# A graph layer on one core: both halves of a pair side by side, eight groups in front, the difference begun on ScalarE and GpSimd

## What is computed

```
summed = segment_sum(x[src], dst)            # sum of the neighbours' rows
aggr   = summed / max(count, 1)
h      = aggr @ W_l.T + b_l + x @ W_r.T
h_norm = (h - mean over rows) * rsqrt(var over rows + 1e-5) * gamma + beta
out    = layernorm(x + relu(h_norm))
```

## Time and profile before

| what | value |
|---|---|
| median of 3 runs | 2656.01 us (2655.27 to 2657.59) |
| the profiled execution | 2652.04 us |
| its span, first to last instruction | 2650.3 us |
| PE busy | 1762.3 us, 66% |
| DVE busy | 1970.0 us, 74% |
| ACT busy | 1466.1 us, 55% |
| POOL busy | 1412.8 us, 53% |
| moved by DMA | 753.48 MB, mean 284 GB/s |

### The profile page before, as it was taken

How to read it: one execution, slowest core, us unless ns; L and a number is a source line. 1 busy time by engine, 2 the same in 40 slices (tenths; PEclk the granted TensorE clock), 3 DMA queues, 4 the chain that set the end, 5 groups by cost and what they waited for, 6 DMA issues and landing times.

```text
span 2650.3 us, 29633 instructions
## 1 busy us (share of the span) xinstructions
PE 1762.3 (66%) x9404; PEld 1421.6 (54%) x9404; DVE 1970.0 (74%) x3465; ACT 1466.1 (55%) x2847; POOL 1412.8 (53%) x688
## 2 busy tenths in 40 slices
PE   5589999999999999999999999997310000000000
PEld 4468777888887777888887777885200000000000
DVE  7735777788887777888887777885688766666666
ACT  3224444455555444555554444543369988888887
POOL 5334554545555555455555554554276656655554
PEclk9789999999999999999999999998655555555555
DMA  4256867888877877888877778888499999999998
GB/s 149 81 159 218 276 230 230 258 257 263 262 251 248 272 257 228 264 249 265 264 245 248 251 256 247 264 253 279 127 366 426 426 426 426 426 426 416 420 420 344
DMA packets 126763, 753.48 MB, mean 284 GB/s; under 512 B 22039, under 2 KB 22039, under 8 KB 66956
## 3 DMA queue, kind: packets, MB, share of 16 engines
q1 hardware_dynamic: 72940, 619.04, 60.7%
q0 software_dynamic: 53664, 132.51, 20.0%
HBM read 515.92 MB, written 246.22 MB: 288 GB/s over the span
## 4 chain that ended last, share of the span: by engine, by line
PE 49%; DMA 26%; DVE 11%; ACT 7%; issue 4%; POOL 2%; SPq 1%; DVEq 0%; POOLq 0%; ACTq 0%
DMA out<-hx 19%; PE pd L533 10%; PE pd L535 10%; PE pd L534 10%; PE pz L638 4%; PE pz L640 4%; PE pz L639 4%; DMA xf<-x,gi 4%; ACT hx L876 3%; ACT hx L886 2%; DVE x_lo L1032 2%; PE px L632 2%; DMA hs<-h_scratch 2%; DVE hot L1038 1%; PE pe L624 1%
## 5 line engine op out<-in xcount | busy, mean ns | idle before, releaser
L1368 POOL DMA_INDIRECT h_scratch<-zz,si x156 | 306.4, 1964 | 683.5 <-ACT zz L790 467.8
L533 PE MATMUL pd<-wc_hi,x_hi 128*128 128x512 f32 x1564 | 639.1, 409 | 40.8 <-POOL x_lo L1295 24.6
L534 PE MATMUL pd<-wc_lo,x_hi 128*128 128x512 f32 x1564 | 617.6, 395 | 7.0 <-issue 7.0
L535 PE MATMUL pd<-wc_hi,x_lo 128*128 128x512 f32 x1564 | 619.1, 396 | 0.0
L1391 POOL TENSOR_TENSOR hx<-hx,scale_b 128x2560 f32<-128x2560 f32 (+2 forms) x91 | 439.5, 4843 | 291.5 <-DMA hx<-h_scratch 250.0
L745 ACT ACTIVATE h_out<-pd 128x512 f32<-128x512 f32 x391 | 233.0, 596 | 403.5 <-PE pd L535 401.9
L533 PEld LDWEIGHTS pd<-wc_hi,x_hi 128*128 128x128 f32 x1564 | 298.3, 191 | 102.4 <-POOL x_lo L1295 24.6
L1320 POOL DMA_INDIRECT xn<-x,gi x156 | 310.3, 1989 | 47.7 <-issue 44.9
L534 PEld LDWEIGHTS pd<-wc_lo,x_hi 128*128 128x128 f32 x1564 | 298.8, 191 | 63.8 <-issue 7.3
L535 PEld LDWEIGHTS pd<-wc_hi,x_lo 128*128 128x128 f32 x1564 | 297.7, 190 | 66.0
L783 ACT ACTIVATE dT_hi<-px 128x512 fp32r<-128x512 f32 x156 | 93.3, 598 | 399.3 <-PE px L632 388.0
(11 more groups left out here) (214 smaller groups left out, 2939.3 us busy)
## 6 DMA issues: line engine op xcount, KB each, us to landing
raw<-xT_whole SPq DMA_DIRECT2D x78, 1280.0 KB
h_scratch<-h_out SPq DMA_DIRECT2D x78, 1280.0 KB
hs<-h_scratch SPq DMA_DIRECT2D x78, 1280.0 KB
hx<-x SPq DMA_DIRECT2D x78, 1280.0 KB, 20.6
hx<-h_scratch SPq DMA_DIRECT2D x77, 1280.0 KB, 15.4
out<-hx SPq DMA_DIRECT2D x77, 1280.0 KB, 18.1
xn<-x,gi POOLq DMA_INDIRECT x156
xf<-x,gi POOLq DMA_INDIRECT x156
```

What stands on the lines that cost most here:

```text
L533: pe.matmul(pd[i][0:n, :], hi, wc["hi"][:, kc, :], start=kc == 0, stop=False)
L534: pe.matmul(pd[i][0:n, :], hi, wc["lo"][:, kc, :], start=False, stop=False)
L535: last = pe.matmul(pd[i][0:n, :], lo, wc["hi"][:, kc, :], start=False, stop=kc == KC - 1)
L1368: pool.indirect_dma_start(out=h_dram[:, :], out_offset=by, in_=zz[:, h, :], in_offset=None, bounds_check=N + 2 * P - 1, oob_is_err=True, c ...
```

## The change

The diff does these things:

- `FRONT` becomes 8. GpSimd splits x for groups up to 8 instead of 4, the small steps of the front move to other places of `between` (rank_extras behind group 6's third product, which is the 33rd; sum_cover behind the 37th), and the turns 0 to 74 hold 341 products instead of 361.
- Each half has its own bank for spreading (`spread_to`) and for transposing (`turned`) and its own `dT_hi`, `dT_lo`. TensorE's order in a turn becomes: spread 0, product, spread 1, product, transpose 0, product, transpose 1, product, correction 0, product, slots, correction 1. The other engines' orders follow.
- `begin` leaves VectorE. ScalarE multiplies `xn` by `ndeg` in place (`scale_own`), and GpSimd adds it to `xf` (`begin`, behind add_z of pair u half 0).
- `copy_z` of half 1 moves to the head of the next turn on ScalarE.
- At the start, `src` and `dst` are loaded from ScalarE's queue, `dst` in rows with one neighbour to either side in place of three shifted copies. The first transposed rows are loaded before the weights, the low part of the weights moves from GpSimd to VectorE, and the first product starts block by block.

Parts that only rename or that belong to the path not taken are left out.

```diff
-FRONT = 4
+FRONT = 8
...
-        dT_hi = sr("dT_hi", [P, KC, P], F32R)
-        dT_lo = sr("dT_lo", [P, KC, P], F32R)
+        dT_hi = [sr(f"dT_hi{h}", [P, KC, P], F32R) for h in range(2)]
+        dT_lo = [sr(f"dT_lo{h}", [P, KC, P], F32R) for h in range(2)]
...
+        spread_to, turned = (pe_, p6), (px, p7)
...
+            load_xT(0)
             for s, w, m in ((s_wl_in, wT_l, 0), (s_wr_in, wT_r, 1)):
                 sp.dma_start(w_raw[:, m], w.rearrange("(c p) f -> p c f", p=P)).then_inc(s, 16)
-            load_xT(0)
...
-                (0, 4): (sum_blocks,),
-                (1, 0): (find_first,),
-                (1, 2): (lambda: pick_windows(0), lambda: pick_windows(1), lambda: pick_windows(2)),
-                (1, 3): (lambda: pick_windows(3), lambda: pick_windows(4)),
-                (1, 4): (lambda: pick_windows(5), lambda: pick_windows(6)),
-                (2, 0): (rank_slots,),
-                (2, 4): (rank_extras,),
-                (3, 3): (sum_cover,),
+                (1, 2): (sum_blocks,),
+                (1, 4): (find_first,),
+                (2, 3): [lambda a=a: pick_windows(a) for a in range(7)],
+                (2, 4): (rank_slots,),
+                (6, 2): (rank_extras,),
+                (7, 1): (sum_cover,),
...
-                if 2 * u + h > 0:
-                    pe.wait_ge(s_d, 2 * u + h)
+                if u > 0:
+                    pe.wait_ge(s_d, 2 * u + h - 1)
                 to = spread[:, h * P:(h + 1) * P]
-                pe.matmul(pe_[:], to, xe_hi[:], start=True, stop=False)
-                pe.matmul(pe_[:], to, xe_lo[:], start=False, stop=True).then_inc(s_e, 1)
+                pe.matmul(spread_to[h][:], to, xe_hi[:], start=True, stop=False)
+                pe.matmul(spread_to[h][:], to, xe_lo[:], start=False, stop=True).then_inc(s_e, 1)
...
                         spread_extras(a, 0)
                     plain(0)
                     if a is not None:
-                        transpose_difference(a, 0)
+                        spread_extras(a, 1)
                     plain(1)
                     if a is not None:
-                        correction(a, 0)
-                        spread_extras(a, 1)
+                        transpose_difference(a, 0)
                     plain(2)
                     if a is not None:
                         transpose_difference(a, 1)
                     plain(3)
                     if a is not None:
-                        correction(a, 1)
+                        correction(a, 0)
+                    plain(4)
                     if u + 2 < U:
                         fill_slots(u + 2)
-                    plain(4)
+                    if a is not None:
+                        correction(a, 1)
...
+            def scale_own(u, h):
+
+                act.wait_ge(s_gn[h], 16 * u + 16)
+                act.wait_ge(s_wgt, u + 1)
+                act.activation(xn[:, h, :], xn[:, h, :], ACT.Copy, scale=ndeg[:, u % 4, h:h + 1]).then_inc(s_own, 1)
...
-                    plain(tiles_at(u - 1)[TG - 1:])
+                    if pair_at(u - 1) is not None:
+                        copy_z(u - 1, 1)
                     if sp_ is not None:
                         for t in range(3, tiles_in(sp_)):
                             square(sp_, t)
+                    plain(tiles[0:2])
                     if a is not None:
                         difference_high(a, 0)
-                    plain(tiles[0:2])
+                    plain(tiles[2:3])
+                    if a is not None:
+                        difference_high(a, 1)
+                    plain(tiles[3:4])
+                    if pair_at(u + 1) is not None:
+                        extras_high(u + 1)
                     if a is not None:
                         copy_z(a, 0)
-                        difference_high(a, 1)
-                    plain(tiles[2:4])
                     if pair_at(u + 1) is not None:
-                        extras_high(u + 1)
+                        scale_own(u + 1, 0)
+                        scale_own(u + 1, 1)
+                    plain(tiles[4:])
                     if s is not None:
                         for t in range(min(3, tiles_in(s))):
                             square(s, t)
-                    if a is not None:
-                        copy_z(a, 1)
...
-            def begin(u, h):
-                dve.wait_ge(s_gn[h], 16 * u + 16)
-                dve.wait_ge(s_gf[h], 16 * u + 16)
-                dve.wait_ge(s_wgt, u + 1)
-                b = u % 2
-                dve.scalar_tensor_tensor(xf[:, b, h, :], xn[:, h, :], ndeg[:, u % 4, h:h + 1], xf[:, b, h, :],
-                                         ALU.mult, ALU.add).then_inc(s_t, 1)
...
                     if p is not None:
                         difference(p, 0)
+                    x_lows(0)
                     if 0 <= u + 2 < U:
                         one_hots(u + 2)
                     if p is not None:
-                        difference_low(p, 0)
-                    x_lows(0)
+                        difference(p, 1)
+                    x_lows(1)
                     if sums_at(u - 1) is not None:
                         take_squares(sums_at(u - 1))
-                    x_lows(1)
                     if p is not None:
-                        difference(p, 1)
+                        difference_low(p, 0)
                     x_lows(2)
                     if p is not None:
                         difference_low(p, 1)
+                    x_lows(3)
                     if sums_at(u) is not None:
                         take_sums(sums_at(u))
                     if pair_at(u + 1) is not None:
                         extras_low(u + 1)
-                        begin(u + 1, 0)
-                        begin(u + 1, 1)
-                    x_lows(3)
+                    x_lows(4)
                     if 0 <= u + 2 < U:
                         indices(u + 2)
...
+                def begin(u, h):
+                    b = u % 2
+                    pool.wait_ge(s_own, 2 * u + h + 1)
+                    pool.wait_ge(s_gf[h], 16 * u + 16)
+                    pool.tensor_tensor(xf[:, b, h, :], xf[:, b, h, :], xn[:, h, :], ALU.add).then_inc(s_t, 1)
...
                     if p is not None:
                         add_z(p, 0)
+                    if pair_at(u + 1) is not None:
+                        begin(u + 1, 0)
+                        begin(u + 1, 1)
```

More of the change, by code:

```diff
@@ L257, in bass_sage_batchnorm_residual_layernorm_kernel @@
         s_go = sem("gather_allowed")
-        s_t, s_xeh, s_xel, s_spread = (sem(n) for n in (
-            "differences_begun", "extras_hi", "extras_lo", "spread_ready"))
+        s_t, s_own, s_xeh, s_xel, s_spread = (sem(n) for n in (
+            "differences_begun", "own_rows_scaled", "extras_hi", "extras_lo", "spread_ready"))
         s_e, s_d, s_x, s_dh, s_dl, s_z, s_ze = (sem(n) for n in (
@@ L753, in copy_window, with blocks @@
                                    banks[a % 3][j][0:EB, 0:HALF], ACT.Copy).then_inc(s_got, 1)
+            act.dma_start(src_i[:, :, 0:EB], src.rearrange("(c b p) -> b c p", b=BP, p=EB)).then_inc(s_src, 16)
+            wide, block = EB + 2, BP * EB
+            def blocks(first, pattern):
+                return bass.AP(dst.tensor, first * EB - 1, [*pattern, [1, wide]])
+            act.wait_ge(s_pad, 1)
+            act.dma_start(dst_i[:, 1:BC - 1, 0:wide], blocks(BP, [[EB, BP], [block, BC - 2]])).then_inc(s_dst, 16)
+            act.dma_start(dst_i[1:BP, 0, 0:wide], blocks(1, [[EB, BP - 1]])).then_inc(s_dst, 16)
+            act.dma_start(dst_i[0:BP - 1, BC - 1, 0:wide], blocks((BC - 1) * BP, [[EB, BP - 1]])).then_inc(s_dst, 16)
+            act.dma_start(dst_i[0:1, 0, 1:wide], dst[0:EB + 1].rearrange("(o p) -> o p", o=1)).then_inc(s_dst, 16)
+            act.dma_start(dst_i[BP - 1:BP, BC - 1, 0:wide - 1], dst[E - EB - 1:E].rearrange("(o p) -> o p", o=1)).then_inc(s_dst, 16)
+            for kc in range(KC):
+                x_high(0, 0, kc)
             for kc in range(KC):
@@ L758, in _ @@
             for kc in range(KC):
-                x_high(0, 0, kc)
-            for kc in range(KC):
                 x_high(1, 1, kc)
-            between = {(1, 2): (0, 1, 2), (1, 3): (3, 4), (1, 4): (5, 6)}
+            between = {(2, 3): range(7)}
             for g in range(FRONT):
@@ L1155, in correct @@
                         dve.wait_ge(s_c[3], TG * g + t + 1)
[L1156 to L1157 removed]
+                        dve.tensor_tensor(dT_lo[0][:, :, 0:m], px[:].rearrange("p (c r) -> p c r", c=KC)[:, :, 0:m],
+                                          dT_hi[0][:, :, 0:m].bitcast(F32), ALU.subtract).then_inc(s_c[4], 1)
                         dve.wait_ge(s_c[5], TG * g + t + 1)
```

86 lines of the change are left out of this document (38 added, 48 removed).

## The result

The changed kernel takes 2673.96 us (median of 4 runs, 2671.69 to 2675.45), the kernel before 2655.64 us on the same chip (4 runs, 2653.08 to 2657.59). The ratio is 1.0069, with a 95% interval of 1.0051 to 1.0086. It is slower by 0.7%, where 2617 us was forecast.

A forecast was written before the change was run, and what follows sets the result against it. It took TensorE's 21.1 us a turn plus a ring of gathers through GpSimd to bound the kernel. Turns -54, front +20, tail -5 made -39, so 2617 us (2580 to 2650; 8 in 10: 2560 to 2662).

The forecast's parts named there:

- 75 x (22.02 - 21.3) = 54 us won: The 75 turns from pair 0 to pair 75: each falls from 22.02 to 21.3 us, 54 us won.
- GpSimd's ring: New ring on GpSimd alone: gathers, landing, addition, z addition, next gathers; 21.5 us in four turns of five.
- part 2: Begin moved to ScalarE and GpSimd: its wait for the last gather makes a new GpSimd ring; turns 21.3 us.
- What sets 22.9 is in GpSimd's timeline and the chain: Slow turns before: a ring of gathers, landing, begin, difference, product, z and gathers sets 22.9 us.
- Part 1: Fewer products and halves side by side: TensorE's floor 20.4 us a turn, waits for dd and dT_lo should go.
- the halves side by side bring nothing: Rival: the ring of gathers keeps 22.0 us a turn and the front only costs; +15, 2671 us, chance 0.07.
- The last sentence of the forecast: Signs of being wrong: landing unlike 7.8 us, GpSimd additions over 2 us, or ScalarE's copies late behind its scaling.
- W + 9.7 us: GpSimd's new ring: W, from z addition's start to last gather's end (taken 11.77 us), plus landing 7.81, addition, two gaps.
- longer than the old ring: Rival: GpSimd's new ring takes 22.7 us a turn with W 12.99; +65 in all, 2721 us, chance 0.12.
- Part 3: The front before pair 0: 20 more products cost 54 us, less savings; 20 us lost, bounds 8 and 35.
- Part 4: The tail, two turns without products behind pair 75: most of four dT_lo waits go, 5 us won.
- The floor: TensorE's own work in a turn with eight groups in front, 4.55 products each: 20.4 us.

The follow-up runs named there:

- a1: The changed kernel with the start of the difference back on VectorE (no ScalarE scaling, no GpSimd addition); 2594.75 us, ratio 0.9774.
- a16: The kernel before with halves side by side, the new start, four groups in front, and gathers issued ahead of half 1's z addition; 2581.93 us.
- b2: The kernel before with the next pair's four gathers issued ahead of the z addition of half 1; 2643.65 us, ratio 0.9956.
- a13: The changed kernel with four groups in front and begin on VectorE, leaving the halves side by side and the new start; 2602.2 us, ratio 0.9809.
- a6: The changed kernel with ScalarE's scaling of half 1 moved into the next turn, behind the z copy of half 1; 2645.5 us, ratio 0.9969.
- a10: The changed kernel with GpSimd's addition over 8 of 512 columns, same waits, incomplete output; 2633.37 us, ratio 0.993.
- a12: The changed kernel with begin on VectorE, gathers first, and two GpSimd additions a turn that nobody waits for; 2595.92 us, ratio 0.9777.
- a14: The changed kernel with begin on VectorE, gathers first, and five idle GpSimd fills of 128x512 in every turn; 2580.98 us, ratio 0.9718.
- a9: The changed kernel with half 1's scaling late and GpSimd's addition over 8 of 512 columns, incomplete output; 2590.46 us, ratio 0.9761.
- b1: The kernel before with only eight groups in front and the new places of the small steps; 2648.27 us, ratio 0.9977.

## Why the prediction was wrong

**Where the miss lies.** The span came out 19.7 us longer, where 39 less were forecast. The front cost 11.0 us for 20, and behind pair 75 3.4 were won for 5. The step that failed is the turns, "75 x (22.02 - 21.3) = 54 us won": measured are 12.1 us lost. The 21.3 rests on GpSimd's ring alone, and puts at nothing what part 2 does to ScalarE's queue and to VectorE. Undoing part 2 gives 79 us (a1).

**What bounds before.** The turn of 22.02 us, TensorE's own 21.1 and the 0.9 between them were read rightly (a16 comes to 21.23). The first wrong step is "What sets 22.9 is in GpSimd's timeline and the chain": b2 took z out of that ring and the turn fell to 21.90 only. The argument went from a ring with the right length, in one stretch, to a cause. VectorE's timeline in that stretch already speaks against it:

```profile
1016.57 0.69 DVE L1071 TENSOR_TENSOR xe_lo<-xe,xe_hi 128x512 fp32r<-128x512 f32 x1 [1.11 <-ACT xe_hi L777]
1017.18 0.35 DVE L1074 TENSOR_SCALAR spread<-iota_f,ct 128x256 fp32r<-128x256 f32 x1
1017.44 1.41 DVE L1066 SCALAR_TENSOR_TENSOR xf<-xn,ndeg,xf 128x512 f32<-128x512 f32 x2
```

VectorE came to its two starts of the difference without standing idle before them. The last gather, which landed at 1017.38, is needed only for the second, which starts some 0.7 us later. The line of all starts says the same (idle time at the end):

```profile
L1066 DVE SCALAR_TENSOR_TENSOR xf<-xn,ndeg,xf 128x512 f32<-128x512 f32 x156 | 111.0, 745 | 7.1 <-issue 5.5 <-DMA xn<-x,gi 0.8 <-DMA xf<-x,gi 0.6
```

If the ring bound, VectorE would stand in front of this instruction until the gathers have landed. It stood 7.1 us in 156 starts, 1.4 of it for gathers. What held the turns was listed in the earlier trace rows and given no term: TensorE's short stops at halves that share one bank (a13).

**Part 1** was taken to remove TensorE's waits, but the sum has no term for it, since there the ring sets the turn. Alone, it is worth 54 us with the early start (a13), 38 of them in the turns. That the waits go is right in the main (dd 30.7 to 8.9 us), that this is worth nothing is wrong. The rival "the halves side by side bring nothing" gave 2671, 3 us from the measured time. That is luck: its mechanism is what a13 refutes.

**Part 2** was to leave the turn at 21.3 us, and costs 79 us. Two terms of it are missing. First, the queue on ScalarE was named (a copy of h, squares, the z copy of half 1) and priced at nothing. Its ring is longer than GpSimd's own: landing, scaling, copy, squares, copy of z, and then the z addition and the gathers. a6 gives 28 us for it. The last sentence of the forecast had it as a sign of being wrong. Second, VectorE was said not to be full and GpSimd's additions were costed by their length on GpSimd (1.28 us; they took 1.70 in the mean and 3.69 at most). What they do to VectorE was left out: 142 us of its busy time, 41 us of the run (a10). The sentence "nothing waits for GpSimd's arithmetic by itself" is not quite true (VectorE's first difference waits 84.7 us in 23 waits for GpSimd's addition). Where it is true, in a12, the additions still cost 16 us.

The Trainium skill has the rule behind the second term. Its page weighed in the forecast, "GPSIMD Engine Reference", says in Specifications that GpSimd shares its SBUF interfaces with VectorE. The Trainium skill, "SBUF — State Buffer", section SBUF: two separate sides, says more: the shared pair is an exclusive lock for a whole instruction. A VectorE operation needs it in a 2-port mode, or with two SBUF inputs; in the second case it conflicts only with a GpSimd operation that reads SBUF. For the operations with two inputs the traces agree: VectorE's start of the difference takes 1.58 us beside the additions of a12 and 0.74 beside the fills of a14. `spread` and `gi` have one SBUF input, so only the 2-port mode could cover them; they were held beside both (`spread` 3.66 us beside the additions of the changed kernel, 0.54 beside the fills), and no run here shows the mode. The forecast took only the factor of two in speed.

**The GpSimd ring**, W + 9.7 us, was there (163.6 us in 61 waits for landings) and did not decide: a9 keeps its waits and is as fast as a1, which leaves them some 8 us at most by the estimate above. Of the rival "longer than the old ring", the sign was right and the mechanism wrong.

**Part 3** was 20 us lost before pair 0, and measured are 11.0. Four groups in front with the new start and order put pair 0 14.1 us earlier (a13), eight put it 24.9 later than that (162.6 to 187.5, a13 to a1). The start's wait fell by 7.0 us (24.6 to 17.6, forecast 9), and the waits for GpSimd's x_lo are 10.0 (forecast 9). One thing was forecast wrongly: the stop of 6.97 us behind the branch did not stay. Neither b1 nor the changed kernel has it, and why it went isn't shown. What was undervalued is the other side: shorter turns bring 26 us back with the old order and 27 with the new one (75 x 0.36, a13 to a1). So eight groups in front are worth some 6 us, not a loss.

**Part 4**: 3.4 us for 5.

**The floor** of 20.4 us a turn is not reached by any kernel; the best has 20.77 with 341 products. The measured parts are 54 us won by part 1 with the start, 7 won by the front (6 by the ratios), 79 lost by part 2, each with the ones before it in place. They add up to 2674, but by construction: they are the steps from before to a13, a1 and the changed kernel.

## What to carry to other kernels

Work moved to GpSimd is not free, even where GpSimd is idle. An elementwise operation there that reads two SBUF operands takes time from VectorE, and that can be more than the move takes off it (142 us for 116 here); compare VectorE's whole busy time before and after. A ring found in the trace is a bound only if cutting it shortens the turn, and many short waits of the bound engine on shared buffers can be worth more than one long chain beside them. When a wait goes onto an engine's queue, put the time of what stands behind it into the sum, even if the engine has room.

## What the runs showed of the hardware

- An addition of 128x512 on GpSimd took 1.27 us at least, 1.70 in the mean and 3.69 at most in the changed kernel. It stretched `spread` from 0.35 to 3.66 us when two came back to back. In the whole run the additions made VectorE busy for 142 us more (a10).
- Fills of the same tile, 636 ns each and 390 of them, changed the time by less than the measurement shows (2580.98 us against 2580.14), and made VectorE busy for 25 us more.
- VectorE also holds GpSimd. In the kernel before, 60 of the 156 gathers of `xn` were issued beside VectorE's additions of 128x2560, which take 2.82 us; these issues took 3.03 us in the median and ended 0.87 after the addition. With VectorE idle the issue took 1.00 us.
- After TensorE's stop of 3.28 us the granted clock was 0.56 in the next 3.5 us, that is mostly the 1.2 GHz level, and 1.00 from 493.5 us on. The matmuls in between came 0.43 us apart. View of windows in the changed kernel (columns as in the earlier trace rows):

```profile
489.00:492.50 3.50, 3.50 (x9) 2.76 (x10) 3.39 (x10) 0.00 (x0) 2.89 (x3) 0.56 0.47 56
493.50:497.50 4.00, 4.00 (x22) 3.33 (x21) 3.67 (x3) 0.87 (x2) 3.39 (x3) 1.00 0.92 285
```
